# Two-layer cross attention on one core: the splitting of layer one's value weights moved behind two row tiles in the opening list

## What is computed

```python
def layer0(x, ctx):                       # 8 heads of 40
    q = heads(x @ w_q)
    z = 0.5 * attend(q, ctx[16:32] @ w_k,      ctx[16:32] @ w_v) \
      + 0.5 * attend(q, ctx[:16]  @ w_k_dis,   ctx[:16]  @ w_v_dis) \
      + 1.0 * attend(q, ctx[-16:] @ w_k_dis,   ctx[-16:] @ w_v_dis)
    return merge(z) @ w_out + b_out + x

def layer1(x, ctx):                       # 20 heads of 16, all 1024 context rows
    q, k, v = heads(x @ Wq), heads(ctx @ Wk), heads(ctx @ Wv)
    p = softmax(q @ k.T / 4)
    return merge(p @ v) @ Wo + bo + x

out = layer1(layer0(x, ctx), ctx)
```

## Time and profile before

| what | value |
|---|---|
| time, median of 3 runs | 325.64 us (325.45 to 331.66) |
| time of the profiled execution | 327.17 us |
| span of the profiled execution | 325.3 us |
| mean granted clock of PE in it | 0.99 |
| busy share of PE, DVE, ACT, POOL | 96%, 81%, 70%, 24% |

### The profile page before, as it was taken

The page is one execution under the profiler, slowest core; times in us unless marked ns, Lnnn a source line. Parts: engine busy times, 40 slices in busy tenths (PEclk is TensorE's granted clock), DMA queues, the critical chain, the costliest instruction groups (busy, mean ns, idle before and its releaser), DMA issues.

```text
span 325.3 us, 6083 instructions
## 1 busy us (share of the span) xinstructions
PE 310.9 (96%) x2086; PEld 167.7 (52%) x2086; DVE 262.0 (81%) x456; ACT 229.2 (70%) x468; POOL 78.4 (24%) x97
## 2 busy tenths in 40 slices
PE   7999997999999999999999999999999999999995
PEld 6678886876667634334343434433334453434324
DVE  1479899779996879989999999999899988893213
ACT  3556455443445778889879878898798876888982
POOL 6065166242434400010014100040441016101030
PEclk9999999899999979999999999999999999999999
DMA  7960008629956741191540915509146111110102
GB/s 219 312 208 0 3 1 210 217 92 157 224 184 209 166 100 55 43 139 33 127 90 34 148 36 114 102 33 151 34 104 104 40 40 38 50 38 28 37 29 82
DMA packets 20193, 32.79 MB, mean 101 GB/s; under 512 B 5539, under 2 KB 9667, under 8 KB 20163
## 3 DMA queue, kind: packets, MB, share of 16 engines
q1 hardware_dynamic: 19075, 31.27, 40.9%
q10 hardware_dynamic: 1088, 1.14, 1.2%
HBM read 20.63 MB, written 11.61 MB: 99 GB/s over the span
## 4 chain that ended last, share of the span: by engine, by line
PE 66%; DVE 11%; ACT 9%; issue 6%; DMA 5%; SPq 3%; POOL 0%; ACTq 0%; DVEq 0%; POOLq 0%
PE ps L1393 19%; PE ps L1370 13%; PE ps L1381 13%; PE ps L1221 10%; PE ps L1042 5%; ACT probs L701 4%; DVE mx L906 3%; ACT probs_last L701 3%; SPq L347 2%; DMA QS<-mT 1%; DMA rec_rows<-recs 1%; DMA xs<-in_x_dram 1%; PE ps L1148 1%; DVE max L845 1%; DMA QS<-q_parts 1%
## 5 line engine op out<-in xcount | busy, mean ns | idle before, releaser
L906 DVE TENSOR_REDUCE mx<-ps 128x1 f32<-128x512 f32 x298 | 186.0, 683 | 17.9 <-PE ps L1370 16.7
L701 ACT ACTIVATE probs<-ps 128x512 f32<-128x512 f32 x216 | 113.5, 609 | 22.3 <-PE ps L1381 20.8
L1370 PE MATMUL ps<-KS,QS 48*128 48x512 f32 x256 | 78.4, 453 | 2.1 <-ACT probs L701 1.2
L1381 PE MATMUL ps<-QS,KS 50*128 50x512 f32 x256 | 72.0, 442 | 1.9 <-DMA QS<-mT 0.9
L1393 PE MATMUL ps<-probs,VS 128*32 128x512 f32 (+1 forms) x552 | 61.0, 517 | 0.3 <-ACT probs L701 0.3
L701 ACT ACTIVATE probs_last<-ps 128x512 f32<-128x512 f32 x104 | 54.7, 608 | 8.3 <-PE ps L1381 7.7
L1370 PEld LDWEIGHTS ps<-KS,QS 48*128 48x128 f32 x256 | 35.3, 185 | 37.6 <-DVE mx L906 17.0
L1381 PEld LDWEIGHTS ps<-QS,KS 50*128 50x128 f32 x256 | 34.1, 187 | 33.4 <-ACT probs L701 13.3
L507 POOL CAST neg_p<-neg 128x16 fp32r<-128x16 f32 x10 | 2.1, 213 | 113.2 <-DVE neg L916 107.6
L1393 PE MATMUL ps<-probs_last,VS 128*32 128x512 f32 (+1 forms) x256 | 29.0, 524 | 0.0
L683 ACT CAST parts<-ps 128x512 fp32r<-128x512 f32 (+1 forms) x18 | 10.5, 585 | 23.6 <-PE ps L1221 23.4
(11 more groups left out here) (186 smaller groups left out, 444.9 us busy)
## 6 DMA issues: line engine op xcount, KB each, us to landing
KS<-k_parts SPq DMA_DIRECT2D x48, 128.0 KB, 4.6
k_parts<-parts SPq DMA_DIRECT2D x8, 512.0 KB, 3.6
QS<-q_parts SPq DMA_DIRECT2D x48, 64.0 KB, 4.7
raw_rows<-o_raw SPq DMA_DIRECT2D x9, 256.0 KB, 2.0
q_parts<-parts SPq DMA_DIRECT2D x4, 512.0 KB, 3.2
cs<-in_ctx_dram SPq DMA_DIRECT2D x2, 768.0 KB, 9.3
KS_last<-k_parts SPq DMA_DIRECT2D x12, 128.0 KB, 4.6
xs<-in_x_dram SPq DMA_DIRECT2D x2, 640.0 KB, 6.5
```

What stands on the lines that cost most here:

```text
L701: act.activation(probs[t % 3][:, h, :], ps[:, bank_of["s", m], :], ACT.Exp, scale=float(D1) ** -0.5).then_inc(exp_done, 1)
L906: dve.tensor_reduce(mx[:, g % BUF, u:u + 1], ps[:, bank_of["m", n], :], AX.X, ALU.max).then_inc(max_done, 1)
L1370: pe.matmul(ps[:, bank, :], QS[g % BUF][rows, pair, qt * P:(qt + 1) * P], KS[g % BUF][rows, pair, half * 512:half * 512 + 512], start=True ...
L1381: pe.matmul(ps[:, bank, :], KS[g % BUF][rows, h // 2, kt * P:(kt + 1) * P], QS[g % BUF][rows, h // 2, :], start=True, stop=True).then_inc( ...
```

## The change

One entry of the list, `("w", 3)`, moves six entries back. Before, it stood between `("x1", 4)` and the loading of the first keys (`("loadk", 0)`, SP alone). Now it stands behind `("x1T", 2)`, `("x1T", 3)`, `("e0", 6)`, `("i0", 6)` and `("s0", 7)`, in front of `("n0", 5)` and the key projection `("k", 0, 1, 1)`. Nothing else differs, and the queues of PE, POOL and SP hold the same rows in the same order.

```diff
-             ("pT", 3), ... ("x1T", 1), ("x1", 4), ("w", 3),
-             ("loadk", 0), ("x1T", 2), ("x1T", 3), ("e0", 6), ("i0", 6), ("s0", 7), ("n0", 5), ("k", 0, 1, 1), ("cT", 4), ("pT", 5),
+             ("pT", 3), ... ("x1T", 1), ("x1", 4),
+             ("loadk", 0), ("x1T", 2), ("x1T", 3), ("e0", 6), ("i0", 6), ("s0", 7), ("w", 3), ("n0", 5), ("k", 0, 1, 1), ("cT", 4), ("pT", 5),
```

## The result

The changed kernel takes 323.17 us in the median (322.64 to 323.93, 5 runs) against 325.64 before; the ratio over the counted executions is 0.9913 with a 95% interval of 0.9893 to 0.9933. That is within 2% of the time before, and clearly faster: the forecast was 322.5 us in a range of 321.1 to 325.4. The profiled execution took 322.64 us against 327.17, its span is 320.5 us against 325.3. Counted executions are those within 1.5% of the fastest of their kernel, the others enter only the medians of whole runs; the profiled execution of the experiment with the filled gap is one of those others, with the clock at 0.50 from 233 to 257 us, and only what lies far ahead of that is read from it.

The account below looks back on a forecast made before the run. DVE's value-weight subtractions ahead of the row tiles' lower parts held PE up. Query start 2.0 + clock 1.66 - new wait 0.3 = 3.35 us, taken as 3.1 after hand-offs: 322.5 us, range 321.1 to 325.4.

Parts of the forecast that it names:

- The lower parts: DVE's last lower part of row tiles 2 and 3, awaited by the query projection, ends at 52.5 us, 3.1 sooner.
- POOL's gain: POOL's bias addition and tile 5 product gain 0.5 us without DVE's subtractions beside them; the query projection starts near 53.75.
- The split in its new place: DVE's three value-weight subtractions, moved behind tile 7's difference, take 1.5 us instead of 3.34 and end at 55.9.
- The new wait: PE, done with the query projections at 57.4 us, waits 0.3 us for tile 5's lower part on DVE.
- ACT: ACT's moved weight copies delay the key projection's copy by 0.6 us, which costs nothing because DVE reads it later.
- Row tile 4's transposes: On PE ahead of the loop, they start near 60.5 us instead of 63.75, 3.25 us sooner, after DVE's tile 5 addition.
- That POOL is the cause: POOL's SBUF work, not DMA traffic, slowed DVE's three value-weight subtractions in the old place: 3.34 us against 1.5.
- The clock: With PE's idle time at most 0.7 us, the query projections run at full clock, saving 1.66 us.
- The rival with the clock term absent: Median runs have no low clock at the query projections, or keep it: gain 1.45 us, 324.2 us; chance 0.31.
- From there each step waits for a step that moved with it: Behind row tile 4's transposes, later steps move along; losing the gain before the loop's first scores would speak against it.
- The low stretch behind 114 us: Rival "more than the sum": this second low-clock stretch is absent too when everything comes 3 us sooner; 320.9 us, chance 0.06.
- the sum: All terms together take 3.1 us off; from the profiled execution's 327.17 us this gives 324.1, off the median 322.5.

Follow-up runs that it names:

- the experiment with the filled gap: Old order plus six extra identity matmuls on PE in its wait for the row tiles' lower parts; 327.26 us, ratio 0.9993 to the old order.
- the run with DVE's share alone: Against the new order, ACT's three value-weight copies go back to their old place, so only DVE's three subtractions stay moved; 323.14 us, ratio 0.9957.
- the run with the split still further back: New order with DVE's value-weight subtractions behind tile 5's probabilities, and POOL's bias additions of tiles 1 to 3 behind its product of tile 7; 323.11 us, ratio 0.9958.
- the two later chips: The unchanged new order run again on the second chip, 323.62 us, ratio 0.9961, and on the third, 323.54 us, ratio 0.9944.

## Why the prediction was right, and where it was off

*The lower parts* end at 52.57 (predicted 52.5). *POOL's gain* was 0.49 us at PE's transposes, 53.75 to 53.26 (0.5), and the query projection starts at 53.56 (53.75; the 0.55 us that the transposes take in the row overlaps the next matmul by 0.25). *The split in its new place* takes 1.40 us, to 55.81 (1.5, to 55.9). *The new wait* is 0.17 us (0.3). *ACT* costs nothing, as the run with DVE's share alone shows from the other side. Row tile 4's transposes come 3.28 us sooner (3.25). Each of these was forecast from rows of before within 0.2 us. One link of the last was not as told: the prediction lets DVE, done with the addition of tile 5 at 60.3, set the start of row tile 4's transposes. In the trace PE comes to them through its own queue without a wait, 2.82 us behind the start of tile 5's sum against 2.70 before, and the place where DVE's work could hold it is POOL's product of tile 7, as the run with the split still further back shows with its 0.46 us. That both ways end near 60.5 is luck.

*That POOL is the cause* was argued from L813's 1.16 us at a DMA share of 0.00. Two runs show it in both directions: with POOL's work moved away the old place costs 1.4 us, with it moved to the new place that costs 3.3. The rule of the Trainium skill that the prediction leaned on (SBUF — State Buffer, "SBUF: two separate sides") sets a DVE instruction with two SBUF inputs against a GpSimd one only if that reads SBUF. The run with the fills agrees: 0.48 us each beside six fills, which write SBUF and read nothing.

*The clock* is the term that was mis-sized. The prediction took 1.66 us off the median, "that the clock does not fall here then". In an execution that loses its clock this is what it costs, 1.66 us between the profiled executions with and without it, and none of the three profiled executions of the new order loses it there. But 51 of 98 executions of the old order never lost it, so the median gets less than the whole term: 2.47 us in place of 3.1 in the first comparison, 1.5 and 2.2 between the medians of the counted executions on the two later chips. The rival with the clock term absent, 1.45 us, describes the full-clock executions, which gain 1.0 and 1.6. The forecast and this rival are thus not two cases of which one holds; both hold, in different executions, and the 1.53 us between the profiled execution and the median was the sign of it. Which of the two numbers the median comes nearer to depends on the chip: the 1.5 us of the second chip is the rival's. That the first comparison came out nearer to the forecast is in part luck, since how often its old order lost the clock is not on record.

*"From there each step waits for a step that moved with it"* is not wholly so: in one profiled execution of the new order out of three the first scores wait 0.58 us for the queries' transfer. The prediction had listed this sign as one that would speak against it. Its weight in the median is below what these runs can tell.

*The low stretch behind 114 us* was absent in all three profiled executions of the new order and present in both of the old order, unchanged. The prediction gave its absence 0.06. So the profiled execution came down by 4.53 us, to 322.64, where the sum gave 324.1. It is no effect of the order that these runs could establish: it came back with the version that stores the key later. In all three traces that have it PE idles at most 0.11 us in any one microsecond from 94 us to its beginning, so the theory that idle time of PE brings the low clock does not cover it. Nothing was tried on it, and its cause stays open.

## What to carry to other kernels

Ahead of moving a slow instruction off the path, ask why it is slow: here it took two and a half times as long as its sibling of the same size, and the answer, another engine's work beside it, offered a second cure that left the order alone. When PE waits for two engines, read what the second wait will be when the first is gone, and whether the first engine's work is what makes the second late. Where a clock can fall behind a wait, as here (1.6 us of wait, 1.7 us of clock), the wait is worth its length or twice that, by execution; look at the spread of the clock over many executions before taking the larger price off a median.

## What the runs showed of the hardware

DVE subtractions with both inputs in SBUF, 320 elements a row, take 0.48 us alone or beside fills by POOL, and 1.02 to 1.20 beside POOL additions or products in SBUF; POOL's instructions lose in turn (1.14 against 0.84, 1.09 against 0.84). With one input in PSUM the DVE instructions L877 and L883 are not slowed, 0.49 and 0.42 us beside POOL additions. The granted clock was 0.50, which is 1.2 GHz, behind waits of PE of 2.1 and 2.5 us in the profiled executions; it was also 0.50 behind 110 to 114 us in three of them, with no such wait ahead. By the mean clock of all counted ones it fell somewhere in 47 of 98 executions of the order with the 2.1 us and in 7 of 8 of the one with the 2.5 us; the heap at 0.995 costs 1.5 to 1.7 us. In the six versions whose waits at that place are at most 0.5 us each it fell in 7 of 79, 1 of 27 in the new order itself.
